# A two-layer transformer step on one core: the scaling of the attention outputs two maxima later, and 71 expert tiles instead of 72

## What is computed

```python
# layer 0: attention with 16 heads of 8, a relative position bias, softmax;
#          feed-forward: 8 experts of 256, each token takes its two best
logits = flat @ router_weight.T + router_bias
topk_w, topk_idx = jax.lax.top_k(softmax(logits), 2)
act = (clip(up) + 1.0) * min(gate, 7) * sigmoid(1.702 * gate)
out = (down(act)[topk_idx] * topk_w).sum()
# layer 1: causal attention; feed-forward: two linear products
new_attn = resid_gain * attn + skip_gain * eye - centre_gain * uniform
out = (new_attn @ v) @ cproj_w
```

## Time and profile before

| | us |
|---|---|
| median of 3 runs | 973.65 (971.24 to 975.08) |
| profiled execution | 975.81 |
| its span, first to last instruction | 974.0 |
| TensorE busy | 780.0 |
| VectorE busy | 644.7 |
| ScalarE busy | 503.4 |
| GpSimd busy | 414.9 |
| steps of the experts | 435 to 615 |
| layer 1, steps with scaling | 730 to 974 |

### The profile page before, as it was taken

The page is one execution under the profiler, slowest core; times in us unless marked ns, Lnnn a source line. Parts: engine busy times, 40 slices in busy tenths (PEclk is TensorE's granted clock), DMA queues, the critical chain, the costliest instruction groups (busy, mean ns, idle before and its releaser), DMA issues.

```text
span 974.0 us, 19905 instructions
## 1 busy us (share of the span) xinstructions
PE 780.0 (80%) x6277; PEld 510.3 (52%) x6278; DVE 644.7 (66%) x1137; ACT 503.4 (52%) x870; POOL 414.9 (43%) x407
## 2 busy tenths in 40 slices
PE   0894796999999999629999999145788989999984
PEld 0752453655555555315555555044566666666663
DVE  6562895898898898515666566373547777676753
ACT  1243253777787776704433334177455555655441
POOL 7006776465656554505777777671201010111000
PEclk9996887999999999859999999666799999999997
DMA  5695744445645542151222221422846465665511
GB/s 144 215 185 135 175 127 116 96 107 119 140 96 127 131 98 63 43 170 43 57 57 54 54 54 46 124 65 56 171 98 157 114 141 137 136 145 131 121 54 51
DMA packets 132670, 106.12 MB, mean 109 GB/s; under 512 B 23317, under 2 KB 124633, under 8 KB 129545
## 3 DMA queue, kind: packets, MB, share of 16 engines
q1 hardware_dynamic: 122348, 91.23, 40.8%
q0 software_dynamic: 4352, 8.99, 3.0%
q10 hardware_dynamic: 5920, 5.24, 1.7%
HBM read 54.60 MB, written 50.03 MB: 107 GB/s over the span
## 4 chain that ended last, share of the span: by engine, by line
PE 30%; DMA 9%; DVE 6%; ACT 4%; issue 4%; SPq 2%; POOL 1%; DVEq 0%; ACTq 0%; POOLq 0%
PE ps L671 8%; DMA od_d<-ev 4%; PE ps L1593 4%; PE ps L692 3%; DVE mx L1297 3%; DMA rec<-od_d 2%; PE ps L673 2%; PE ps L683 2%; PE ps L665 2%; PE ps L1602 1%; ACT rows L893 1%; PE ps L1545 1%; PE ps L1571 1%; PE ps L1543 1%; SPq L1115 1%
## 5 line engine op out<-in xcount | busy, mean ns | idle before, releaser
L1297 DVE TENSOR_REDUCE mx<-ps 128x4 f32<-128x1024 f32 (+1 forms) x224 | 265.9, 1210 | 121.2 <-PE ps L1545 55.9
L1448 ACT ACTIVATE probs<-probs 128x1024 f32<-128x1024 f32 x128 | 131.9, 1053 | 72.3 <-DVE probs L1307 62.4
L1453 ACT ACTIVATE probs<-ps 128x1024 f32<-128x1024 f32 x96 | 96.8, 1023 | 85.2 <-PE ps L1571 57.8
L1219 POOL TENSOR_TENSOR qkr<-qkf,qk 128x512 f32<-128x512 f32 x27 | 31.2, 1156 | 228.1 <-ACT qk L1417 228.1
L1593 PE MATMUL ps<-probs,vpad 128*32 128x256 f32 (+1 forms) x2048 | 121.7, 368 | 8.1 <-ACT probs L1448 7.6
L1247 POOL TENSOR_TENSOR probs<-probs,tabB 128x1024 f32<-128x1024 f32 x42 | 99.3, 2367 | 56.8 <-ACT probs L1460 56.8
L1537 PE MATMUL ps<-tabA,eyeb 128*128 128x512 bf16 x256 | 101.3, 396 | 17.1 <-DMA ks<-parts_d 11.3
L1307 DVE TENSOR_TENSOR probs<-ps,tabB 128x1024 f32<-128x1024 f32 x86 | 100.6, 1214 | 13.4 <-PE ps L1565 13.4
L1539 PE MATMUL ps<-ks,qs 96*128 96x256 bf16 x512 | 101.5, 280 | 0.0
L671 PE MATMUL ps<-qs,probs 128*128 x144 | 81.0, 645 | 1.4
L1593 PEld LDWEIGHTS ps<-probs,vpad 128*32 128x32 f32 x2048 | 56.1, 112 | 49.4 <-issue 22.9
(11 more groups left out here) (227 smaller groups left out, 1519.1 us busy)
## 6 DMA issues: line engine op xcount, KB each, us to landing
parts_d<-qk SPq DMA_DIRECT2D x64, 192.0 KB, 4.4
qs<-parts_d SPq DMA_DIRECT2D x32, 384.0 KB, 5.0
ks<-parts_d SPq DMA_DIRECT2D x32, 384.0 KB, 6.7
parts_d<-qk SPq DMA_DIRECT2D x64, 128.0 KB, 3.3
od_d<-ev SPq DMA_DIRECT2D x64, 128.0 KB
slots_in<-probs SPq DMA_DIRECT2D x1, 4680.0 KB
probs<-slots_in SPq DMA_DIRECT2D x72, 65.0 KB, 1.8
parts_d<-qk SPq DMA_DIRECT2D x64, 64.0 KB, 1.9
```

Source lines behind the costliest of these rows:

```text
L1297: nc.vector.tensor_reduce(mx[:, s.buf(), t, heads[0]:heads[-1] + 1], ring[:, slot].rearrange("p (h n) -> p h n", n=w), AX.X, ALU.max).then ...
L1448: nc.scalar.activation(probs[:, j, :], probs[:, j, :], ACT.Exp).then_inc(exp_done, 1)
L1453: nc.scalar.activation(probs[:, j, :], ring[:, slot], ACT.Exp).then_inc(exp_done, 1)
```

## The change

Two things are changed. In layer 1 `scale` stands at position 5 instead of 2: behind the maxima of A0 to A3 instead of behind those of A0 and A1. And there are 71 places of 128 rows for the experts instead of 72: 8192 rows in groups of 8 experts, each padded to full tiles, take at most (8192 + 8 · 127) // 128 = 71 tiles. The loop of the experts has seven rounds instead of eight, and the steps 63 to 70 become straight-line code.

```diff
-SLOT_TILES = NT * TOPK + E
+SLOT_TILES = (NT * TOPK * P + E * (P - 1)) // P
@@ experts
     def run(eng, body):
-        pipeline(eng, body, -1, 7, 8, SLOT_TILES + 3, FLIGHT, SLOT_TILES)
+        pipeline(eng, body, -1, 7, 7, SLOT_TILES + 3, FLIGHT, SLOT_TILES)
@@ experts, sync
         for b in range(4):
-            sp.wait_ge(y_store[b], 16 * (SLOT_TILES // 4))
+            sp.wait_ge(y_store[b], 16 * ((SLOT_TILES + 3 - b) // 4))
@@ attention
-    SCALE, INVERT, PROJECT = (2, 7, 10) if layer else (9, 15, 11)
+    SCALE, INVERT, PROJECT = (5, 7, 10) if layer else (9, 15, 11)
```

## The result

| | before | changed |
|---|---|---|
| median of 22 runs, us | 975.06 | 970.31 |
| lowest to highest | 971.24 to 981.11 | 965.38 to 975.76 |
| profiled span | 974.0 | 965.9 |

The ratio is 0.9946, with an interval of 0.9928 to 0.9964: 5.3 us faster, between 3.5 and 7.0. The forecast was 968.5, which is 5.1 us less than the median known then; the range was 965.0 to 972.4. The measured median lies 1.8 us above the forecast, and 1.4 of that is the median of the kernel before, which came out at 975.06 with 22 runs instead of 973.65 with three.

The account below looks back on a forecast made before the run. Bounds: in layer 1 a DMA chain and a VectorE chain of nearly equal length ending at the reciprocal, in the experts TensorE with its sequencer. 3.5 + 1.6 = 5.1 us less gave 968.5 us against the median, range 965.0 to 972.4.

Parts of the forecast that it names:

- What bounds each place: Layer 1: DMA and VectorE chains ending at the reciprocal; experts: TensorE with its sequencer, 2.0 us a straight-line tile, 2.4 looped.
- the two chains: Layer 1: output stores' landing then load of softmax sums, and VectorE's chain through the scaling, both ending at the reciprocal.
- The experts' 3.5 us: Experts: tile 62 to the last tile takes 17.7 us instead of 21.17, by one tile fewer and straight-line steps.
- the second loads: Experts: tiles 64 to 66 behind the loop load their owner once more, 0.6 us each on top of 2.0.
- The scaling's cost of nothing: Layer 1: behind A3's maximum the scaling is hidden in VectorE's 1.55 us wait for A4; uncovered it would cost 1.3 us.
- VectorE ready 1.26 us earlier: Layer 1: with the scaling moved, B1 begins 1.26 us earlier and VectorE is ready for the reciprocal as much earlier.
- The scaling's 1.6 us: Layer 1: gain from moving the scaling, only where the sums' landing leaves room; 1.6 us less, bounds 0 and 3.2.
- the forecast's six terms: Layer 1: gains in six steps, 0.63, 0.19, 0.06, 0.19, 0.12 and 0.39 us, summing to 1.6 us.
- A: Layer 1: the scaling's chain is the real bound; 1.26 us off in each of eleven steps, 955.5 us in all; chance 0.10.
- B: Nothing gained in layer 1 and straight-line tiles no faster; only the tile, 1.9 us, 971.7 us; chance 0.19.
- C: Experts: straight-line tiles run behind their code, up to 2.97 us each; 1.0 us slower in all, 974.7 us; chance 0.08.
- D: Layer 1: another wait stands ahead of A2, the move does nothing; 3.5 us alone, 970.2 us; chance 0.63 together with the forecast.

Follow-up runs that it names:

- e4: Changed kernel with layer 1's reciprocal at position 8 instead of 7, behind A5's maximum; 960.29 us, 0.9835 of the kernel before.
- e5: Changed kernel with SyncE's stores of the attention outputs ahead of the first parts' stores in layer 1; 0.9831 of the kernel before.
- e1: Changed kernel with the scaling back at position 2, so 71 tiles and seven rounds alone; 0.9958 of the kernel before.
- e3: Kernel before with seven rounds of the experts' loop instead of eight, all 72 tiles kept, scaling at 2; 0.9957 of the kernel before.
- e6: Changed kernel with the attention outputs' stores ahead of the first parts' stores in layer 1 and the scaling at position 2; 0.9930 of the kernel before.
- e2: Kernel before with only the scaling moved to position 5, 72 tiles and eight rounds kept; 0.9961 of the kernel before.
- e10_rounds_1: Changed kernel with one round of the experts' loop instead of seven, tiles 15 to 70 straight-line; 0.9712 of the kernel before.

## Why the prediction was right, and where it was not

**What bounds each place.** Right in both. In layer 1 the two chains were of nearly the same length; every reciprocal but the first and the last of the twelve-step stretch now stands for the sums (0.26 to 1.42 us, 0.7 in the mean, where about 1 was forecast), and `e4` and `e5`, two different ways to take that wait away, both gave what the move of the scaling could not.

**The experts' 3.5 us.** Right in sum (3.56) and in each term: the tile, the straight-line steps, the second loads at 0.5 us each where I took 0.6. The traces of `e1` and `e3` show the two halves apart, their times do not.

**The scaling's cost of nothing.** Right: it lies in VectorE's wait for A4, 1.03 us of which are left. It was held by GpSimd's second rest, as worked out, and took 0.88 us.

**VectorE ready 1.26 us earlier.** Mis-sized: 0.84 us in the step above. Counted from the start of A1's maximum, B1 comes 1.3 us earlier (2.41 instead of 3.70 us behind it), but A4's maximum only 0.84: it began at 798.75, 5.49 us behind 793.26, where before it was 798.76 to 805.09, 6.33. What took the rest is the wait of L1630 for ScalarE's copy, which the prediction did not have. In the old order that copy was done at 802.04, 1.0 us ahead of the weights. From the kernel before, VectorE's maximum A1, ScalarE's copy and TensorE's weights:

```profile
798.76 1.23 DVE L1297 TENSOR_REDUCE mx<-ps 128x4 f32<-128x1024 f32 x1 [0.30 <-PE ps L1545]
...
801.61 0.43 ACT L1432 ACTIVATE vpad<-ps 128x128 f32<-128x128 f32 x2
...
803.03 0.30 PEld L1630 LDWEIGHTS ps<-xnT,wvs 128*128 128x128 f32 x2
```

It made little difference to the sum, since the landing took nearly all of it anyway. With the stores first and the copy at its old place the move is worth 0.7 to 0.9 us in eight of the twelve steps (`e5` and `e6`), close to this 0.84.

**The scaling's 1.6 us.** That it is small is shown; its size is not, and its sign only by the runs of `e2`. The twelve steps took 196.1, 198.6, 197.7 and 200.9 us in the four profiled executions that have the scaling at 5, the reciprocal at 7 and the stores in the old order, and 198.1, 198.2 and 197.8 in the three that have it at 2. The first of the forecast's six terms, 0.63, lies in the step ahead of these twelve; with it the thirteen take 214.1, 214.4, 213.9 and 217.0 us against 215.5, 215.7 and 214.4. The traces together thus show no clear gain in those steps; the runs of `e2` show 3.8 us with an interval from 2.1 to 5.4, but those of `e3`, against the same runs of the kernel before, also show 2.5 us more than its trace has a place for. The whole change less the experts' part alone is 0.9946 against 0.9958, 1.2 us, within the noise of either. I can't settle between these, and since the 1.6 isn't shown, it is in part luck that the whole came out at 5.3 us where 5.1 was forecast. A single execution can't settle it: the landing of the output stores took 3.9 to 5.1 us in ten steps of one execution of the changed kernel (746 to 901 us), and up to 6.2 in `e10_rounds_1`, and with the scaling at 5 nothing else covers that. My landings were those of one execution, and I took the distances of 0.06 to 0.63 us in it for properties of the steps. That they were small was right; to add them up to a tenth was more than they bear.

**The rivals.** A (all of the 1.26 us in every step) fell; once the stores are first, the scaling's chain is the bound, but for 0.8 to 0.9 us a step. B (only the tile) fell with the trace of `e3`. C (straight-line code late) fell with `e10_rounds_1`. D (the wait ahead of A2 has another reason, so that the move does nothing) fell with the pair of `e5` and `e6`: TensorE's 15.2 us for A2's maximum in the second are 2.9 in the first. The Trainium skill (Advanced Engine Details and Errata, section ISA Cache) gives an instruction cache two lines of 256 instructions, and names a larger one for TensorE; it states sizes alone. What the prediction made of them, a possible cost for the engines with short loop bodies, did not show: with 56 tiles more of straight-line code in `e10_rounds_1` the tiles stood 2.0 us apart. The range held.

## What to carry to other kernels

When an instruction is moved out of a chain, look for the second chain that ends at the same place, and measure how far behind it is before pricing the move; if it is a DMA's landing, shorten that first (an earlier issue, or work put ahead of the wait), and the move then pays. A hardware loop is not free, above all where its body has to reload what straight-line code would hold: compare the distance of equal steps in the prologue and in the loop. On a queue that waits in order, the price of putting a transfer ahead is the wait of everything behind it, not the transfer.

## What was not expected of the hardware

The tiles were 2.4 us apart in the loop and 2.0 in straight-line code with the same products, and 56 tiles more of straight-line code brought no visible cost: 31 blocks of the first instruction queue were loaded in the changed kernel, 38 with one round. And two profiled executions of nearly the same program differed by 7 us of TensorE's busy time in layer 0, at a mean granted clock of 0.90 and 0.92 of 2.4 GHz, more than the whole change. So the time itself varies with the execution: of the 22 runs of the changed kernel the five fastest (965.4 to 965.7 us) had a mean granted clock of 0.929 to 0.931, the six slowest (972.7 to 975.8 us) one of 0.915 to 0.919.
